# A transformer layer on eight cores: x's load cut in two halves on two queues, FFN weight buffers three to two

## The reference, cut to what matters

```python
# x: [8, 4096, 1024] float32, 16 heads of 64, FFN width 4096
def attn(x):
    q, k, v = split(x @ w_qkv.T)
    a = softmax(einsum('bhid,bhjd->bhij', q, k) / 64)
    return merge_heads(a @ v) @ w_out.T + b_out

def ffn(x):
    h = silu((x @ w1.T) * s1) * ((x @ w2.T) * s2)    # 1024 -> 4096
    h = gelu((h @ h1.T) * h1s)                       # 4096 -> 4096
    h = gelu((h @ h2.T) * h2s)                       # 4096 -> 4096
    return (h @ w3.T) * w3s                          # 4096 -> 1024

x = x + layernorm(attn(layernorm(x)))
x = x + layernorm(ffn(layernorm(x)))
```

## Time and profile before

| | us |
|---|---|
| runs before | 8725.89 and 8856.51, median 8791.2 |
| profiled execution | 8688.41 |
| its span, slowest core | 8686.9 (all cores 8666.5 to 8686.9) |
| mean granted TensorE clock | 0.93 on every core |
| first loop / attention / FFN (from the stages' borders) | 559 / 2928 / 5180 |

### The profile page before, as it was taken

The page is one execution under the profiler, slowest core; times in us unless marked ns, Lnnn a source line. Parts: engine busy times, 40 slices in busy tenths (PEclk is TensorE's granted clock), DMA queues, the critical chain, the costliest instruction groups (busy, mean ns, idle before and its releaser), DMA issues.

```text
span 8686.9 us, 99842 instructions; the slowest of 8 cores (8666.5 to 8686.9 us)
## 1 busy us (share of the span) xinstructions
PE 7877.0 (91%) x33664; PEld 3145.0 (36%) x33664; DVE 1173.9 (14%) x1693; ACT 2766.6 (32%) x3286; POOL 361.9 (4%) x644
## 2 busy tenths in 40 slices
PE   6879788888988888899998999998999998999997
PEld 2332222222222222344443444443444443444443
DVE  2310212112121121200001200002200002200002
ACT  1248677776767766110010111010111010111100
POOL 0000000000000000100000100000100000100000
PEclk8888888888888888899999999999999999999998
DMA  4110111111011110554446554445554445544445
GB/s 102 63 53 30 44 39 40 39 44 44 30 49 40 44 44 30 86 94 76 78 75 115 86 95 74 77 78 109 88 94 76 75 78 110 89 83 73 78 78 114
DMA packets 155660, 611.53 MB, mean 70 GB/s; under 512 B 13744, under 2 KB 21936, under 8 KB 105904
## 3 DMA queue, kind: packets, MB, share of 16 engines
q0 software_dynamic: 98304, 453.03, 29.1%
q1 hardware_dynamic: 56880, 152.13, 5.3%
HBM read 957.42 MB, written 58.72 MB: 117 GB/s over the span
## 4 chain that ended last, share of the span: by engine, by line
PE 55%; DMA 2%; DVE 1%; issue 0%; ACT 0%; DVEq 0%; SPq 0%; ACTq 0%; POOLq 0%
PE psA L231 11%; PE psA L236 11%; PE psB L231 11%; PE psB L236 11%; PE ps L210 4%; PE psC L231 1%; PE psC L236 1%; DMA x1c<-x_sc 1%; PE ps L236 1%; PE ps L231 1%; DMA stg<-w_s 0%; DVE ffn_sb L840 0%; DMA out_f<-ffn_sb 0%; DVE tmp_sb L836 0%; DMA ln2q<-ln_sc 0%
## 5 line engine op out<-in xcount | busy, mean ns | idle before, releaser
L503 PE MATMUL ps<-e_sb,v_sb 128*65 128x512 bf16 x4096 | 1221.3, 410 | 98.8 <-ACT e_sb L486 96.2
L486 ACT ACTIVATE e_sb<-psA 128x1024 bf16<-128x1024 f32 x809 | 878.5, 1086 | 335.9 <-PE psA L210 333.7
L486 ACT ACTIVATE e_sb<-psB 128x1024 bf16<-128x1024 f32 x809 | 883.7, 1092 | 163.7 <-PE psB L210 163.7
L231 PE MATMUL psA<-h_sb,stg 128*128 128x512 bf16 x2048 | 781.2, 381 | 14.3 <-DVE h_sb L685 9.7
L231 PE MATMUL psA<-h1o_sb,stg 128*128 128x512 bf16 x2048 | 776.2, 379 | 7.5 <-ACT h1o_sb L708 7.5
L236 PE MATMUL psA<-h_sb,stg 128*128 128x512 bf16 x2048 | 781.1, 381 | 0.0
L231 PE MATMUL psB<-h_sb,stg 128*128 128x512 bf16 x2048 | 776.2, 379 | 0.0
L236 PE MATMUL psB<-h_sb,stg 128*128 128x512 bf16 x2048 | 776.2, 379 | 0.0
L231 PE MATMUL psB<-h1o_sb,stg 128*128 128x512 bf16 x2048 | 776.2, 379 | 0.0
L236 PE MATMUL psB<-h1o_sb,stg 128*128 128x512 bf16 x2048 | 776.2, 379 | 0.0
L236 PE MATMUL psA<-h1o_sb,stg 128*128 128x512 bf16 x2048 | 776.2, 379 | 0.0
(11 more groups left out here) (131 smaller groups left out, 7379.5 us busy)
## 6 DMA issues: line engine op xcount, KB each, us to landing
stg<-h_s POOLq DMA_DIRECT2D x256, 1024.0 KB, 8.7
k_sb<-k_sc SPq DMA_DIRECT2D x65, 1024.0 KB, 5.5
stg<-w_s POOLq DMA_DIRECT2D x256, 256.0 KB, 4.1
stg<-w_s POOLq DMA_DIRECT2D x64, 1024.0 KB, 10.0
xt<-x_f SPq DMA_DIRECT2D x16, 2048.0 KB, 12.3
x_sc<-xt POOLq DMA_DIRECT2D x8, 2048.0 KB, 8.6
x1c<-x_sc SPq DMA_DIRECT2D x64, 256.0 KB, 5.3
out_f<-ffn_sb SPq DMA_DIRECT2D x8, 2048.0 KB, 7.2
```

What stands on the lines that cost most here:

```text
L231: lambda e, o=oa, l=l, r=ra, st=st, sp=sp: e.matmul(o, l, r, start=st, stop=sp, skip_group_check=True),
L486: lambda e, eb=eb, ps=psS: e.activation(out=eb[:], in_=ps[:], func=AF.Exp, scale=1.0 / 64),
L503: st=(tk == 0), sp=(tk == TKT - 1): e.matmul(o, l, r, start=st, stop=sp, skip_group_check=True),
```

## The change

It does three things.

First, the load of x in `emit_ln1` becomes two loads of 1 MB, the first four of the eight column blocks by SP and the other four by ScalarE, with the same semaphore and the same `Buf`. Second, the staging buffers of the FFN become two: tile oj of h1, h2 and w3 uses buffer oj % 2 and its load waits for the matmuls of tile oj - 2. Third, the argument `at_waits` of the two matmul helpers, which no call gives, and two semaphores of the third buffer go.

```diff
@@ -376,8 +370,12 @@
-                    dma("sync", DMA_SEMS[f"xt{j % 2}"], xb[:].rearrange("p (c t) -> p c t", t=512),
-                        x_3d[:, :, j * 512:(j + 1) * 512], wbufs=[xbuf])
+                    dma("sync", DMA_SEMS[f"xt{j % 2}"],
+                        xb[:, 0:2048].rearrange("p (c t) -> p c t", t=512),
+                        x_3d[:, 0:4, j * 512:(j + 1) * 512], wbufs=[xbuf])
+                    dma("scalar", DMA_SEMS[f"xt{j % 2}"],
+                        xb[:, 2048:4096].rearrange("p (c t) -> p c t", t=512),
+                        x_3d[:, 4:8, j * 512:(j + 1) * 512], wbufs=[xbuf])
                     layer_norm(xb, xbuf, sq_sb[:], B("sq1"),
@@ -640,7 +638,7 @@
             stg = [ctxC.enter_context(nc.sbuf_tensor(f"stg{i}", [128, 4096], BF16))
-                   for i in range(3)]
+                   for i in range(2)]
@@ -691,11 +689,10 @@
                 def h_stage(w_staged, scale_sb, scale_buf, in_sb, in_buf, out_sb, out_buf):
                     for oj in range(KF):
-                        sl = oj % 3
-                        sg = stg[sl]
-                        sgb = B(f"stg{sl}a")
-                        dma("gpsimd", DMA_SEMS[f"stg{sl}a"], sg[:], w_staged[oj],
-                            wbufs=[sgb, B(f"stg{sl}b")])
+                        sg = stg[oj % 2]
+                        sgb = B(f"stg{oj % 2}a")
+                        dma("gpsimd", DMA_SEMS[f"stg{oj % 2}a"], sg[:], w_staged[oj],
+                            wbufs=[sgb, B(f"stg{oj % 2}b")])
@@ -761,11 +758,10 @@
                     for oj in range(KD):
-                        sl = oj % 3
-                        sg = stg[sl]
-                        sgb = B(f"stg{sl}a")
-                        dma("gpsimd", DMA_SEMS[f"stg{sl}a"], sg[:], w3_s[oj],
-                            wbufs=[sgb, B(f"stg{sl}b")])
+                        sg = stg[oj % 2]
+                        sgb = B(f"stg{oj % 2}a")
+                        dma("gpsimd", DMA_SEMS[f"stg{oj % 2}a"], sg[:], w3_s[oj],
+                            wbufs=[sgb, B(f"stg{oj % 2}b")])
```

More of the change, by code:

```diff
@@ L126, in build_program @@
         for nm in ("cst", "wq", "wo", "xt0", "xt1", "qb0", "qb1", "kb0", "kb1",
-                   "ln2q", "x1r", "stg0a", "stg0b", "stg1a", "stg1b", "stg2a", "stg2b",
+                   "ln2q", "x1r", "stg0a", "stg0b", "stg1a", "stg1b",
                    "spq", "spk", "spx1", "spln2", "spout"):
@@ L195, in op, with mm_group @@
             return tok
-        def mm_group(items, out_buf, rbufs, extra_waits=(), tp=None, at_waits=None):
+        def mm_group(items, out_buf, rbufs, extra_waits=(), tp=None):
             waits = list(extra_waits)
@@ L205, in mm_group @@
                 st, sp = (i == 0), (i == n - 1)
-                w_i = list(waits) if i == 0 else []
-                if at_waits and i in at_waits:
-                    w_i += [w for w in at_waits[i] if w is not None]
                 tok = P.add("tensor",
@@ L211, in mm_group @@
                                 o, l, r, start=st, stop=sp, tile_position=tp),
-                            waits=w_i, incs=[sPE] if sp else [])
+                            waits=waits if i == 0 else (), incs=[sPE] if sp else [])
             for b in rbufs:
@@ L216, in mm_group, with mm_group2 @@
             return tok
-        def mm_group2(items2, out_a, out_b, rbufs, extra_waits=(), at_waits=None):
+        def mm_group2(items2, out_a, out_b, rbufs, extra_waits=()):
             waits = list(extra_waits)
@@ L232, in mm_group2 @@
                                   o, l, r, start=st, stop=sp, skip_group_check=True),
-                              waits=w_i,
+                              waits=list(waits) if i == 0 else (),
                               incs=[sPE] if sp else [])
```

## The result

| | before | after |
|---|---|---|
| profiled execution, us | 8688.41 | 8786.13 |
| spans of the cores, us | 8666.5 to 8686.9 | 8759.1 to 8784.5 |
| mean granted TensorE clock | 0.93 on every core | 0.93 on every core |
| fastest run in this comparison | 8687.77 (of 10) | 8777.02 (of 13) |
| median of all runs | 8953.83 | 8929.32 |

The ratio after/before is 1.0093, with a 95% interval of 1.0067 to 1.0119. The change makes the kernel slower by 0.9%, some 80 us. That is less than the 2% from which the forecast counted a change, and more than the measurement's own uncertainty.

The account below looks back on a forecast made before the run. TensorE's chain was taken as the bound (55% of the span, DMA 2%), so only later matmul starts cost. 8688.4 + 67 + 4 + 42 = 8801 us; 8850 was named, range 8760 to 8990.

Parts of the forecast that it names:

- The sum: Whole kernel: profiled 8688.4 us plus 67 for first-loop steps, 4 at kernel start, 42 in w3, giving 8801, +1.3%.
- the named number: Whole kernel: 8850 us, the middle between 8801 on the profiled time and 8904 on the median of shown runs.
- the x steps: First loop, j=1 to 7: Square waits for ScalarE's half of x, 9.6 us seven times, 67 us (48 to 88).
- the start: At j=0: second half of x lands later and layer norm decides the first Q matmul, +4 us (0 to 12).
- only x: Rival: only the x load costs, w3 stalls vanish or are swallowed by the out_f wait; 8759 us, chance 0.12.
- only buffers: Rival: only the staging buffers cost, second x half issued ahead of Square's turn; 8730 us, chance 0.03.
- Landing 7.3: First-loop step: ScalarE's 1 MB x half meets the k_sc store and lands in 7.3 us (5.5 to 9.2).
- A longer chain behind the landing: First-loop step: from x's landing to the first L323 takes longer than from Square today, 1.8 us (1.3 to 2.5).
- w3: 42 us forecast: w3, two buffers: five stalls of 2.5 us a round, net 10.6 a round, four rounds, 42 us (20 to 70).
- The give-back: w3: unstacked loads return 0.7 us a round on stg waits and 1 on x1c reads.
- The clock rival: w3: landings above 9.8 us make stalls pass 3 us and drop TensorE's clock; 8894 us, over 2% slower, chance 0.15.
- Faster: Rival: thinner DMA queue frees 52 us of x1c and stg waits and both costs vanish; 8636 us, chance 0.02.

Follow-up runs that it names:

- x_only: Kernel before with only the x edit (halves on SP and ScalarE), three staging buffers; ratio 1.0046, first-loop step 71.8 us.
- buf_only: Kernel before with only the buffer edit (two staging buffers in h1, h2 and w3), x as before; ratio 1.0068, w3 40.4 us longer.
- x_halves_sp: Kernel before with x in two halves, both issued by SP one after the other, three staging buffers; ratio 0.9983, steps 65.0 us.
- x_all_act: Kernel before with the whole 2 MB x load issued by ScalarE as one DMA, three staging buffers; first-loop step 78.3 us, 65.0 before.
- x_eighth_act: Kernel before with seven of x's eight blocks loaded by SP, one (256 KB) by ScalarE, three staging buffers; first-loop step 68.4 us.
- x_two_bufs_b: Changed kernel's x halves with separate semaphores, not waiting for each other, three staging buffers; steps 71.8 us, first Q matmul at 57.6 us median.
- best: Kernel before with V evicted by ScalarE, slice 1's load held, w3 weights in halves, more PSUM tiles and x1c buffers, blockwise out_f stores; 8530.14 us against 8692.75.
- w3_two: Kernel before with two staging buffers in w3 only, three in h1 and h2; w3 710.3 us, +44.6.
- w3_one: Kernel before with one staging buffer in w3, three in h1 and h2; tiles 18.9 us (median), w3 1224 us.

## Why the prediction was right and wrong, point by point

**The sum.** It gave 8801 us on the profiled time; the profiled execution took 8786 and comparable runs 8777 to 8786. The two mechanisms and their places were as described. The sum was 15 us high, and the named number, 8850, 64 us above the profiled execution. As changes: the sum asked for 113 us, the named number for 162, and the runs gave 80 to 98. That the sum comes out so near is in part luck: its largest term, the x steps, was 20 us too high, the start and w3 together 4 too low, and attention gave back 4 that no term had.

**Where the number came from.** This is the step that failed. The forecast added half the distance between the profiled execution and the median of two earlier runs, 49 us. That distance is no property of the kernel: the fastest run of before in this comparison is 8687.8, the profiled time of before within 1 us. The sum belonged on the profiled time. Behind it comes the one term that was well off, the 67 us for the x steps (below). The range, 8760 to 8990, holds both the comparable runs and the median of all, since it starts from "only x" on the profiled time. Its parts don't all follow: the low end, 48+4+20, takes the start at its middle and not at 0, and the 90 of the high end is neither of the two ends given for w3, 70 and 102. Neither changes what follows.

**What can be told from no change.** The forecast took about 2% as the least difference that a measurement shows. The measured interval is 0.26% to either side here, and 0.4 to 0.65% in the comparisons of x_only, buf_only and x_halves_sp. By the first bound all of the forecast's own cases but the last are plainly slower: the sum itself, +1.3%, was five intervals from zero. By the others "only buffers", +0.5%, could not be told from no change. The chances rested on too coarse a resolution, not on the wrong mechanism.

**The x steps: 67 us forecast, 47 to 48 measured.** 9.6 per step against 6.8, just inside the low end of 48. Term by term:

- Issue 0.5: measured 0. The issue takes 0.39 us but runs beside the last kt copy (97.60 beside 97.53 to 98.11).
- Landing 7.3: about 6.1. The gap from the last kt copy's end to Square grew from -0.1 to 6.0 us, a mean over 56 steps (7.56 of idle in the step shown). The half met the k_sc store, as forecast, but was not held up in proportion; the store was, 7.7 instead of 4.7. "Shared wholly" was the wrong model for the load at this size. For 2 MB it was nearer the truth (8.5 to 10.7 by core before, 11.7 to 13.0 in x_all_act).
- A longer chain behind the landing, 1.8: measured 0.7 (from Square to the first operation that writes the normalised slice, L317 now and L323 before: 12.33 us, 11.67 before, means). The value came from j=0, which differs by more than the idle time of TensorE; the earlier trace rows was the wrong place to read it.

The page of the Trainium skill cited in the prediction (DMA: Bandwidth & Descriptors, Anatomy of one DMA) would have 4.4 us for this half. The page gives its fit for DMAs of GpSimd's path; these loads go through ScalarE's and SP's queues, which the prediction doesn't say. The trace has 6.0 to 6.2, between the page's figure and the forecast's; for 256 KB the page's formula gives 2.6 and x_eighth_act shows 3.5 in the median. The total by it, 47 us, agrees with the 47 to 48 measured only because its short landing and the forecast's long issue and chain cancel.

**The start: +4 forecast (0 to 12), +5.6 measured.** The order of events was right: first half landed and second issued at 24.9 (18.6 by the forecast's halving), 17 us of landing (14 to 18 forecast), and the layer norm decides instead of the last weight. The landing came 7.7 us later in the median of the cores. That lies inside the forecast's 2 to 8 by luck: half of 28.6 and 14 to 18 make 28 to 32, which is 0 to 4 us later, and the halving was 6 us too short, since the first half, 1 MB, takes about 20 us among the weights. The last weight landed 4.2 us sooner where about 6 was argued. x_two_bufs_b shows the serial pair as the cause, and x_halves_sp, a serial pair on one queue, has the same late casts (38.5 to 40.4).

The rule of the Trainium skill's front page (Trainium Kernel Development and Optimization, Key Constraints), that spreading DMAs over issuing engines saves issue time alone, was taken to mean that no gain is to be had at the start. In the steps the runs agree with it. At the start they don't bear that reading out: by the medians of the cores, with the two halves free of each other the cast starts 6 us before that of the kernel before, and with slice 0 alone on ScalarE's queue 12 us before. Part of that is the issue time the rule speaks of: ScalarE issues at 1.1 us, SP at 3.9 to 4.3 behind six small loads. The rest isn't issue time alone: in x_two_bufs_b ScalarE's half, issued at 1.1, lands in 7.3 to 10.4 us, and SP's, issued at 4.7 to 7.9, in 20.7 to 23.2. Between these two issues come the first of the 24 weight loads, which POOL issues from 1.6 us on, so whether the queue or the place ahead of the weights does it isn't told apart. SP's queue holds slice 1's load as well, but best, where that load is held back, left the cast at 32 to 34, so sharing SP's queue with it isn't the explanation.

**h1 and h2: 0 forecast, +0.1 of 3559 measured.** The cover of 13.8 us held against landings of 8.3 to 9.2, as the earlier trace rows said.

**w3: 42 us forecast, 44.4 measured.** A pair of tiles took 17.12 us, the forecast's 7.80+9.3=17.1, against 14.57 before. That the two agree to the hundredth is luck. L was taken as 9.3; over all 1 MB loads of w3 it is 9.0 in the mean, and 8.8 in the loads that a stalled tile waited for. The difference is made up by 0.36 us from landing to the first matmul, which the sum had at nothing, by a mean of 0.54 instead of 0.49 to the issue, and, for the remaining 0.1, by the few stalled tiles that ran at the lower clock (last section). In the first half of a round the seven gaps grew from 52.1 to 59.3 us in all (forecast: three stalls), the last four gaps of the second half from 29.3 to 34.9 (two), 12.8 a round where 12.3 was forecast. That every second tile pays and the next pays nothing was right for few of the pairs: mostly both come late, nearly eight stalls of 1.4 us a round in place of five of 2.5. The give-back, 1.7 a round, is 1.7 as what remains (12.8 less 11.1). Its parts were not as argued: VectorE's waits for x1c went from 44.0 to 23.6 us on core 7, from 48.2 to 21.5 on core 3 and from 38.3 to 42.5 on core 0, so they scatter by more than the 1 us a round argued for, and what of them reached the end isn't told by these rows.

**What was to be seen.** Confirmed: the 1 MB load on ScalarE's queue, the 10.7 us of idle before the sum matmuls, the first loop's end, h tiles at their length. Square starts 6.0 us after the last kt copy in the mean, not 7 to 8. The alternating tiles are there in part of the half rounds only. "TensorE waiting on stg near 50 us in all" was wrong as a marker: 17.8 to 35.3 us stand under stg on the three cores read, and the rest under ffn_sb, qs_sb and cs_sb. None of the signs of being wrong came: the half lands in 6.2, w3's tiles aren't at 7.32, and w3's granted clock is 0.91 (core 0, 4690 to 4860).

**The rivals.** "Only x" falls with w3_two, where the buffers alone cost 44.6 us, and "only buffers" with x_only. The clock rival falls: of the 320 loads that can make a tile late, 16 took over 9.8 us, and the busy time of w3's matmuls grew by 3.5 us only. (Loads whose wait is covered took up to 13.5.) w3_one shows that its mechanism is real at 9 us of idle. "Faster" falls: no 1 MB load of w3 landed in under 8.0, where it needed 6.84.

**Left open.** Attention is 3.9 us shorter after the change and 4.5 in x_only, 1.5 in buf_only; what gives that back wasn't followed.

## What to carry to other kernels

A DMA issued from a compute engine's list costs its landing whenever its consumer is the next operation of that list: place the issue a stage ahead of its use, and let only an idle queue prefetch late. Compare issue plus landing with the compute that covers them, stage by stage: two buffers cost nothing at 13.8 us a tile and 2.5 us for every pair of tiles at 7.3, and two half loads cured what a third whole buffer was there for. Put the sum on the profiled time, and ask what the measurement can resolve before calling 1% no change.

## What the runs showed that was not expected

The granted clock can fall after a shorter idle than the earlier trace rows shows. TensorE of core 0 in the changed kernel, and the six microseconds after (PE, PE loads, VectorE, ScalarE and POOL busy, clock, DMA share, GB/s):

```profile
4710.34 8.75 PE L207 MATMUL ps<-h_sb,stg 128*128 128x512 bf16 x32 [2.07 <-DVE qs_sb L784]
```

```profile
4710.00:4716.00 6.00, 5.66 (x19) 2.30 (x20) 0.19 (x1) 0.00 (x0) 0.00 (x0) 0.72 0.87 153
```

After 2.07 us of idle the clock was 0.72, where 2.44 us had left it at 1.00. Over the eight cores 17 of the 249 stalled tiles of w3 ran longer in this way, behind 1.9 to 3.8 us of idle, and others behind up to 3.6 us did not. So the length of the last gap alone doesn't tell which of the two levels (1.2 or 2.4 GHz) follows. It cost little: the stalled tile ran 8.75 us instead of 7.07, and over all of w3 the matmuls were busy 3.5 us longer.

A load and a store that meet don't share the loss alike: the 1 MB load of x took 6.2 us and the 1 MB store 7.7, where the store takes 4.7 without it. When the whole 2 MB meet the store (x_all_act, core 3), the load takes 12.2 instead of 10.4 and the store 11.3.
